# Layer 2 of a four-layer graph network: VectorE's compares of unit u + 2 ahead of its sum and add of unit u

## The chip, the cores and the metric

One core of a Trainium2 chip runs the whole program. The metric is the time of one execution on the device in microseconds (us), the median over runs. Engines are named as in the profile: PE is TensorE's matmul and PEld its weight load, DVE is VectorE, ACT is ScalarE, POOL is GpSimd and SP is SyncE; a q behind the name (PEldq, DVEq) marks what the engine's own instruction sequencer does, register work above all.

## The reference

A graph network of four layers over 6250 nodes and 206250 edges, 128 features for each node. The change touches layer 2 alone, a mean over neighbours:

```python
def _L2_gnn_ref(x, edge_index, Wl, bl, Wr, br):
    tgt, nbr = edge_index[0], edge_index[1]
    agg_sum = segment_sum(x[nbr], tgt, n)
    deg = segment_sum(ones(E), tgt, n)
    agg = agg_sum / maximum(deg, 1.0)[:, None]
    out = relu(x @ Wl + bl + agg @ Wr + br)
    ...
h = maximum(_layernorm(x), 0.0)
x = x + _L2_gnn_ref(h, edge_index, ...)
```

The kernel computes `agg_sum` and `deg` in `l2_edges`, as matrix products.

## The kernel before

The program is a row of phases with a barrier of all engines between them. The nodes lie in NB = 49 blocks of 128, and the edges are sorted into tiles of 128. A tile and a block that it touches make a meeting; there are NMEET = 4896 of them (padding included). `l2_edges` handles them in units of U = IG = 16 meetings with the same source block, so in 306 units, and a unit in two halves of H = 8. Its loop has 153 iterations of two units on each engine. `g` counts halves (612) and `u` units. Per unit:

- VectorE, `hot_of` (L2041): two compares of 128x2048 bf16 build 16 pairs of one-hot matrices, `hot_dst` and `hot_src`, from the edge ends in `ends_of`. Both tiles have two buffers. It raises `hot`.
- TensorE, `build` (L2014): for a half, 8 matmuls of a one-hot pair, 128x128 each, into PSUM `psM`. It raises `built`.
- ScalarE (L2003): one copy of a half from `psM` to `meets` in bf16. It raises `moved`.
- TensorE, `apply` (L2018 to L2025): one register load of 8 block numbers from `dst_blk` (L2018), then 8 matmuls of 390 columns with a block of `parts` each, whose address comes from a register; they add up in one bank of PSUM `psO`. It raises `summed`.
- VectorE: the sum of the three parts of the unit's `psO` bank into `sums` (L2060, it raises `joined`), and the add of `sums` onto the block of `agg` (L2064, it raises `added`). The block numbers for both units of an iteration are loaded from `src_blk` into VectorE's registers at the head of its loop (L2052).

The order of the work is written out by hand: each engine runs its own list in order, and semaphores join them. TensorE's list is build(g+1), apply(g), so its matmuls of a half are always built one half ahead of use. build(g+1) waits for `hot` when g+1 is the first half of a unit; apply(g) waits for ScalarE's copy of g, and in the first half of a unit for `joined`, so that the bank of `psO` is free. VectorE's list is, for unit u: compares of unit u+1, then sum of u, then add of u. The sum has to wait for `summed` of both halves of u.

No DMA runs in this phase: both number tables and `parts` are in SBUF.

Of the kernel before, what the change touches and what calls it, by code (L numbers as in the profile page):

```python
# [4 lines left out]
F32 = mybir.dt.float32  # L5
I32 = mybir.dt.int32
BF16 = mybir.dt.bfloat16
# [3 lines left out]
ENG = mybir.EngineType  # L11


P = 128
N, E, D = 6250, 206250, 128
HEADS, HEAD_DIM = 4, 32
NB = -(-N // P)
# [11 lines left out]
NTX = NT + 4 * HALF  # L29
# [4 lines left out]
QC = NPX // P  # L34
# [10 lines left out]
IG = 16  # L45
NMEET = 4896
JR = 40
NJ = JR * P
TPP = NTX // P
XW = D + 2  # L50
assert NMEET % (2 * IG) == 0 and NMEET >= NTX + (NB - 1) * NB + (IG - 1) * NB and NJ >= NMEET + IG and NTX % P == 0 and QC * 2 == TPP
LN_EPS = 1e-5
assert (P * ET - E) <= HALF * P and NH % 2 == 0 and NPX % P == 0 and ET * P >= E + 2 * P
BLOCK_RANGE = "block numbers are clamped to 0..NB-1 where they are made"
# [5 lines left out]
def fresh(kind):  # L60

    _names[0] += 1
    return f"{kind}_{_names[0]}"
# [41 lines left out]
def bc(ap, shape):  # L105
    return ap.broadcast_to(shape)


def flat(ap):
    return ap.rearrange("p a b -> p (a b)")  # L110


def gnn_kernel(nc, ins, out):
# [24 lines left out]
    with es:  # L138
# [27 lines left out]
        with nc.sbuf_tensor([P, NB, W], F32) as agg:  # L166
            c["agg"] = agg
            l1_finish(nc, c, ins, table1, running, last_pairs)
            with nc.sbuf_tensor([P, 2, NJ], BF16) as ends_of, nc.sbuf_tensor([1, NJ], I32) as dst_blk, nc.sbuf_tensor([1, NJ // IG], I32) as src_blk:
                l2_lists(nc, c, qtab, tile_rows, starts, meet_rows, ends_of, dst_blk, src_blk)  # L170
                with nc.sbuf_tensor([P, NB, 3, XW], BF16) as parts:
                    l2_nodes(nc, c, parts)
                    l2_edges(nc, c, ends_of, dst_blk, src_blk, parts)
            l2_finish(nc, c, ins)
# [1802 lines left out]
def l2_edges(nc, c, ends_of, dst_blk, src_blk, parts):  # L1977

    es = ExitStack()
    sb = lambda shape, dt=F32: es.enter_context(nc.sbuf_tensor(fresh("buf"), shape, dt))
    sem = PhaseSemaphores(nc)
    es.callback(sem.give_back)
    agg = c["agg"]
    U, H = IG, IG // 2
    with es:
        iota, sums = sb([P, P, 2], BF16), sb([P, 2, XW])
        hot_dst, hot_src = sb([P, 2, U // 2, P, 2], BF16), sb([P, 2, U // 2, P, 2], BF16)
        meets = sb([P, 2, H, P], BF16)  # L1990
        psM = es.enter_context(nc.psum_tensor(fresh("psum"), [P, 2, H, P], F32))
        psO = es.enter_context(nc.psum_tensor(fresh("psum"), [P, 2, 512], F32))
        numbered, hot, built, moved, summed, joined, added = (sem() for _ in range(7))
        with nc.Block() as block:
            @block.scalar
            def _(act):
                act.sem_inc(moved, 2)
                with act.Fori(0, NMEET // (2 * U)) as i:
                    for h in range(4):
                        g = 4 * i + h  # L2000
                        act.wait_ge(built, g + 1)
                        act.wait_ge(summed, g + 1)
                        nc.scalar.copy(meets[:, h % 2].rearrange("p a k -> p (a k)"), psM[:, h % 2].rearrange("p a k -> p (a k)")).then_inc(moved, 1)  # L2003

            @block.tensor
            def _(pe):
                def build(g, h, u):
                    if h % 2 == 0:
                        pe.wait_ge(hot, u + 1)
                    pe.wait_ge(moved, g + 1)  # L2010
                    b = (h // 2) % 2
                    for k in range(H):
                        at = H * (h % 2) + k
                        last = nc.tensor.matmul(psM[:, h % 2, k, :], hot_dst[:, b, at // 2, :, at % 2], hot_src[:, b, at // 2, :, at % 2], start=True, stop=True)  # L2014
                    last.then_inc(built, 1)

                def apply(g, h, u, i):
                    blocks = nc.values_load_multi_w_load_instructions(  # L2018
                        dst_blk[0:1, bass.ds(2 * U * i + H * h, H)], engines=[ENG.PE], min_val=0, max_val=NB - 1,
                        skip_runtime_bounds_check_because=BLOCK_RANGE)[1]  # L2020
                    pe.wait_ge(moved, g + 3)
                    if h % 2 == 0:
                        pe.wait_ge(joined, u + 1)
                    for k in range(H):
                        last = nc.tensor.matmul(psO[:, (h // 2) % 2, 0:3 * XW], meets[:, h % 2, k, :], parts[:, bass.ds(blocks[k], 1), :, :].rearrange("p b w d -> p (b w d)"),  # L2025
                                                start=(h % 2 == 0 and k == 0), stop=(h % 2 == 1 and k == H - 1))
                    last.then_inc(summed, 1)

                pe.sem_inc(summed, 2)
                build(0, 0, 0)  # L2030
                with pe.Fori(0, NMEET // (2 * U)) as i:
                    for h in range(4):
                        g = 4 * i + h
                        build(g + 1, h + 1, 2 * i + (h + 1) // 2)
                        apply(g, h, 2 * i + h // 2, i)

            @block.vector
            def _(dve):
                def hot_of(b, at):
                    for to, w in ((hot_dst, 0), (hot_src, 1)):  # L2040
                        last = nc.vector.tensor_tensor(to[:, b], bc(iota[:].unsqueeze(1), [P, U // 2, P, 2]),  # L2041
                                                       bc(ends_of[:, w, at].rearrange("p (a t) -> p a t", t=2).unsqueeze(2), [P, U // 2, P, 2]), ALU.is_equal)
                    last.then_inc(hot, 1)

                dve.sem_inc(added, 1)
                dve.sem_inc(joined, 2)
                nc.vector.memset(agg[:], 0.0).then_inc(added, 1)
                nc.vector.tensor_copy(iota[:], bc(c["iota"][:].unsqueeze(2), [P, P, 2])).then_inc(numbered, 1)
                dve.wait_ge(numbered, 1)
                hot_of(0, slice(0, U))  # L2050
                with dve.Fori(0, NMEET // (2 * U)) as i:
                    blocks = nc.values_load_multi_w_load_instructions(  # L2052
                        src_blk[0:1, bass.ds(2 * i, 2)], engines=[ENG.DVE], min_val=0, max_val=NB - 1,
                        skip_runtime_bounds_check_because=BLOCK_RANGE)[1]
                    for h in range(2):
                        u = 2 * i + h
                        dve.wait_ge(built, 2 * u)
                        hot_of((h + 1) % 2, bass.ds(2 * U * i + U * (h + 1), U))
                        dve.wait_ge(summed, 2 * u + 4)
                        nc.vector.tensor_reduce(sums[:, h, :], psO[:, h, 0:3 * XW].rearrange("p (w d) -> p d w", w=3), AX.X, ALU.add).then_inc(joined, 1)  # L2060
                        dve.wait_ge(joined, u + 3)
                        dve.wait_ge(added, u + 2)
                        a = flat(agg[:, bass.ds(blocks[h], 1), 0:D + 1])
                        nc.vector.tensor_tensor(a, a, sums[:, h, 0:D + 1], ALU.add).then_inc(added, 1)  # L2064
# [568 lines left out]
```

## Time and profile before

| | us |
|---|---|
| median of 3 runs | 11218.07 |
| lowest and highest | 11213.9, 11227.5 |
| the profiled execution | 11216.49 |
| its span, first to last instruction | 11214.7 |
| the layer 2 edge phase, 6530 to 8622 us of the span | 2092.0 |
| TensorE busy in it | 1428.16 |
| VectorE busy in it | 978.34 |
| ScalarE busy in it | 619.51 |

The span is that of one profiled execution, and all rows come from it. TensorE's granted clock is given as a share of 2.4 GHz; a single stretch is at one of two levels, 1.0 (2.4 GHz) or 0.5 (1.2 GHz), and a mean lies between them.

### The profile page before, as it was taken

The numbers are of one execution on the slowest core, as the hardware profiler recorded it, in microseconds if no ns is written. First come the engines' busy times: TensorE is split into PE (matmuls) and PEld (weight loads), VectorE is DVE, ScalarE is ACT, GpSimd is POOL, SyncE is SP. The second block draws the span as 40 slices with busy tenths as digits, with TensorE's granted clock in tenths as the row PEclk, the third lists the DMA queues.
The fourth block names the chain that finished last, engine by engine and source line by source line (L and its number), as shares of the span: only waits on it lengthen the run. The fifth ranks groups of instructions, "written<-read, shape, count | busy, mean of one in ns | idle before, by whom it ended". The sixth has DMA issues, their size and how long they took to land. (4 is left out here: it accounts for less than half of the span.)

```text
span 11214.7 us, 161449 instructions
## 1 busy us (share of the span) xinstructions
PE 7016.7 (63%) x46023; PEld 5941.3 (53%) x46024; DVE 6329.4 (56%) x14524; ACT 2694.6 (24%) x4442; POOL 5210.9 (46%) x5267
## 2 busy tenths in 40 slices
PE   0034334443567658878787456666666588888885
PEld 0033333333466646666666334444444588888885
DVE  8932222222577766666666444444445566666665
ACT  5022222222455532222222132222222100000000
POOL 0057777777100057777777300000000477777773
PEclk5566666666678779999999779989898566666665
DMA  4045545545444445555555500000000333333335
GB/s 153 0 144 157 157 155 158 157 155 168 116 111 114 110 127 149 154 156 148 154 149 156 96 10 0 0 0 0 0 0 1 83 103 107 103 104 107 103 105 86
DMA packets 1150492, 1136.52 MB, mean 101 GB/s; under 512 B 239363, under 2 KB 959825, under 8 KB 1150117
## 3 DMA queue, kind: packets, MB, share of 16 engines
q1 hardware_dynamic: 948422, 666.82, 21.2%
q0 software_dynamic: 195904, 465.66, 15.2%
q10 hardware_dynamic: 6048, 2.84, 0.1%
q14 instruction: 89, 0.73, 0.0%
q8 instruction: 29, 0.48, 0.0%
HBM read 731.30 MB, written 403.51 MB: 101 GB/s over the span
## 5 line engine op out<-in xcount | busy, mean ns | idle before, releaser
L1028 POOL DMA_INDIRECT buf<-node_rows,buf x1728 | 1743.9, 1009 | 527.4 <-issue 526.2
L1522 POOL DMA_INDIRECT buf<-node_rows_ln,buf x1728 | 1711.4, 990 | 561.2 <-issue 496.9
L694 POOL DMA_INDIRECT edge_rows_by_src<-buf x1728 | 1692.6, 979 | 551.5 <-issue 526.4
L1058 PE MATMUL psum<-buf 128*128 128x128 f32 x1728 | 375.3, 375 | 1296.5 <-DVE buf L1021 1293.6
L2025 PE MATMUL psum<-parts,buf 128*128 x4896 | 1068.1, 368 | 141.4 <-issue 97.0
L2175 POOL IOTA buf<- 49x1 f32 x1 | 0.1, 124 | 2244.4 <-POOLq L821 2244.4
L1058 PEld LDWEIGHTS psum<-buf 128*128 128x128 f32 x1728 | 304.8, 199 | 1316.8 <-issue 1316.8
L2003 ACT CAST buf<-psum 128x1024 bf16<-128x1024 f32 x612 | 619.5, 1012 | 1475.7 <-PE psum L2014 1475.7
L786 DVE COPY buf<-buf 128x32 int32<-128x32 int32 x108 | 20.1, 186 | 1465.7 <-DMA buf<-records_by_dst 1465.5
L2041 DVE TENSOR_TENSOR buf<-buf,ends_of 128x2048 bf16<-128x2048 bf16 x614 | 724.6, 1222 | 134.5 <-issue 134.4
L2014 PE MATMUL psum<-buf 128*128 128x128 bf16 x4904 | 431.9, 235 | 569.0 <-DVE buf L2041 569.0
L2025 PEld LDWEIGHTS psum<-parts,buf 128*128 128x128 bf16 x4896 | 513.3, 106 | 518.4 <-issue 332.8
L2405 PE MATMUL psum<-buf 128*128 128x5 f32 x3456 | 744.3, 353 | 50.1 <-ACT buf L2382 50.1
L2405 PEld LDWEIGHTS psum<-buf 128*128 128x128 f32 x3456 | 734.7, 327 | 64.1 <-ACT buf L2382 64.1
L2014 PEld LDWEIGHTS psum<-buf 128*128 128x128 bf16 x4904 | 344.0, 106 | 767.6 <-DVE buf L2041 688.4
L2060 DVE TENSOR_REDUCE buf<-psum 128x130 f32<-128x390 f32 x306 | 172.6, 564 | 921.5 <-PE psum L2025 921.5
L2413 PE MATMUL psum<-buf 128*128 128x132 f32 x3456 | 662.0, 377 | 27.1 <-DVE buf L2497 26.7
L2413 PEld LDWEIGHTS psum<-buf 128*128 128x128 f32 x3456 | 646.8, 288 | 29.0 <-issue 28.8
L1633 DVE TENSOR_TENSOR buf<-buf 128x512 f32<-128x512 f32 x432 | 298.5, 691 | 623.5 <-DMA buf<-node_rows_ln,buf 597.4
L1537 ACT ACTIVATE buf<-psum 128x512 f32<-128x512 f32 x432 | 257.9, 597 | 1542.1 <-PE psum L1572 1506.3
L1568 PE MATMUL psum<-buf 128*128 128x128 f32 x1728 | 293.7, 297 | 511.8 <-DVE buf L1633 511.0
L1584 PEld LDWEIGHTS psum<-buf 128*128 128x128 f32 x3456 | 485.8, 203 | 239.9 <-issue 239.9
(428 smaller groups left out, 14529.8 us busy)
## 6 DMA issues: line engine op xcount, KB each, us to landing
buf<-edge_rows_by_src SPq DMA_DIRECT2D x114, 1056.0 KB, 5.7
buf<-edge_rows_by_src SPq DMA_DIRECT2D x110, 1024.0 KB
buf<-in_edge_attr SPq DMA_DIRECT2D x864, 128.0 KB
running_weighted_sums<-buf SPq DMA_DIRECT2D x108, 544.0 KB, 3.5
buf<-loc_rows_by_src SPq DMA_DIRECT2D x110, 512.0 KB, 5.0
buf<-loc_rows_by_dst SPq DMA_DIRECT2D x110, 512.0 KB, 4.8
running_sums<-buf SPq DMA_DIRECT2D x108, 512.0 KB, 3.0
edge_rows_by_src<-buf SPq DMA_DIRECT2D x139, 260.0 KB, 2.7
```

The lines of the kernel that those rows point to most:

```text
L694: nc.gpsimd.indirect_dma_start(rows, bass.IndirectOffsetOnAxis(ap=at[:, h, t:t + 1], axis=0), st[:, h, t, :], None).then_inc(scattered[h], 16)
L1028: nc.gpsimd.indirect_dma_start(rows[:, t, 0:used], None, table, bass.IndirectOffsetOnAxis(ap=stage[:, t:t + 1], axis=0)).then_inc(sem, 16)
L1058: last = nc.tensor.transpose(psT[:, sg % 2, t * P:(t + 1) * P], oh[:, 4 * sg + t, :], c["ident"][:])
L1522: nc.gpsimd.indirect_dma_start(xn[:, j, t, :], None, table1, bass.IndirectOffsetOnAxis(ap=stage[:, j // 4, at:at + 1], axis=0)).then_inc(g ...
L1584: last = nc.tensor.matmul(psT[:, (j + 1) % 2, t * P:(t + 1) * P], hS[:, (j + 1) % 2, t * P:(t + 1) * P], w2[:], start=True, stop=True)
L1633: nc.vector.tensor_tensor(ea[:, g4], ea[:, g4], xn[:, g4], ALU.add).then_inc(partial, 1)
L2003: nc.scalar.copy(meets[:, h % 2].rearrange("p a k -> p (a k)"), psM[:, h % 2].rearrange("p a k -> p (a k)")).then_inc(moved, 1)
L2014: last = nc.tensor.matmul(psM[:, h % 2, k, :], hot_dst[:, b, at // 2, :, at % 2], hot_src[:, b, at // 2, :, at % 2], start=True, stop=True)
L2025: last = nc.tensor.matmul(psO[:, (h // 2) % 2, 0:3 * XW], meets[:, h % 2, k, :], parts[:, bass.ds(blocks[k], 1), :, :].rearrange("p b w d ...
L2041: last = nc.vector.tensor_tensor(to[:, b], bc(iota[:].unsqueeze(1), [P, U // 2, P, 2]), bc(ends_of[:, w, at].rearrange("p (a t) -> p a t", ...
L2405: last = nc.tensor.matmul(psS[:, q, :], oh[:, s, 2 * q + k, :], sel[:, b, 2 * q + k, :], start=(k == 0), stop=(k == 1))
L2413: last = nc.tensor.matmul(sums(q), oh[:, h, 2 * q + k, :], rows[:, h, 2 * q + k, :], start=(k == 0), stop=(k == 1))
```

## The change

Before its loop VectorE builds two units of one-hot matrices instead of one, and in the loop, at unit u, the compares are those of u + 2. These go into the buffers that unit u itself has used, so they wait until TensorE has built both halves of u (`built` at 2u + 2, where it was 2u). The sum and the add of u stand behind them, as the sum and the add of u stood behind the compares of u + 1. The number of buffers, R, is 2 as before; all other edits put R in place of a 2 and 2R in place of a 4. The list `ends_of` is read one unit further at the end, which the assertion covers; two compares more are issued in all.

```diff
-    U, H = IG, IG // 2
+    U, H, R = IG, IG // 2, 2
@@ block.vector
-                dve.sem_inc(joined, 2)
+                dve.sem_inc(joined, R)
...
                 hot_of(0, slice(0, U))
-                with dve.Fori(0, NMEET // (2 * U)) as i:
+                hot_of(1, slice(U, 2 * U))
+                with dve.Fori(0, NMEET // (R * U)) as i:
...
-                    for h in range(2):
-                        u = 2 * i + h
-                        dve.wait_ge(built, 2 * u)
-                        hot_of((h + 1) % 2, bass.ds(2 * U * i + U * (h + 1), U))
+                    for h in range(R):
+                        u = R * i + h
+                        dve.wait_ge(built, 2 * u + 2)
+                        hot_of((h + 2) % R, bass.ds(R * U * i + U * (h + 2), U))
                         dve.wait_ge(summed, 2 * u + 4)
                         nc.vector.tensor_reduce(sums[:, h, :], psO[:, h, 0:3 * XW]...
-                        dve.wait_ge(joined, u + 3)
+                        dve.wait_ge(joined, u + 1 + R)
```

The first place is VectorE's list ahead of its loop and the first unit in it. L2041 is `hot_of`; in the kernel after, lines behind it stand one further down (L2052 is L2053, L2060 is L2061, L2064 is L2065). What moved:

```order
 L2048 CAST buf<-buf 128x256
-L2041 TENSOR_TENSOR buf<-buf,ends_of 128x2048 x2
-L2051 UNCONDITIONAL_BRANCH
-L2051 ISA
-L2052 TENSOR_LOAD src_blk
-L2057 REGISTER_ALU
+L2041 TENSOR_TENSOR buf<-buf,ends_of 128x2048 x4
+L2052 UNCONDITIONAL_BRANCH
+L2052 ISA
+L2053 TENSOR_LOAD src_blk
+L2058 ISA
```

Two compares, those of unit 1, are now ahead of the loop, and so all compares in the loop belong to a unit later than before.

The second place is the first unit in the body of VectorE's loop, with the semaphores that rows wait for: sem_274 is `built`, sem_276 `summed`, sem_277 `joined`, sem_278 `added`. The kernel before:

```order
L2052 TENSOR_LOAD src_blk
L2057 REGISTER_ALU
L2041 ISA [waits sem_274]
L2041 TENSOR_TENSOR buf<-buf,ends_of 128x2048
L2041 ISA
L2041 TENSOR_TENSOR buf<-buf,ends_of 128x2048
L2059 REGISTER_ALU
L2060 TENSOR_REDUCE buf<-psum 128x130 [waits sem_276]
```

The kernel after:

```order
L2053 TENSOR_LOAD src_blk
L2058 ISA
L2041 ISA [waits sem_274]
L2041 TENSOR_TENSOR buf<-buf,ends_of 128x2048
L2041 ISA
L2041 TENSOR_TENSOR buf<-buf,ends_of 128x2048
L2060 REGISTER_ALU
L2061 TENSOR_REDUCE buf<-psum 128x130 [waits sem_276]
```

The rows are the same but for the register step that works out the value to wait for (L2057, now L2058), and what they stand for is not: the pair of compares is that of u + 2 instead of u + 1, and the value of `built` that the first row waits for is 2u + 2 instead of 2u.

TensorE's list is the same in both kernels. Its part from one build to the apply behind it (sem_275 is `moved`, sem_161 `hot`):

```order
L2009 REGISTER_ALU
L2014 MATMUL psum<-buf 128x128 [waits sem_275,sem_161]
L2014 MATMUL psum<-buf 128x128 x7
L2018 ISA
L2018 TENSOR_LOAD dst_blk
L2021 REGISTER_ALU
L2025 ISA [waits sem_275]
L2025 MATMUL psum<-parts,buf 128x390
```

Nothing moved here: the first matmul of a unit's build waits for `hot`, and the register load stands between a build and its apply.

## Rows read from the trace of the kernel before

**Rows 1.** The page: span, and granted clock in 40 slices.

```profile
span 11214.7 us, 161449 instructions
...
PEclk5566666666678779999999779989898566666665
```

**Rows 2.** The windows view of the layer 2 edge phase: length, busy time (instructions), clock, DMA.

```profile
core 0: us, PE busy (x) PEld busy (x) DVE busy (x) ACT busy (x) POOL busy (x), PEclk, DMA share, GB/s
6530.00:8622.00 2092.00, 1428.16 (x9800) 852.54 (x9800) 978.34 (x1228) 619.51 (x612) 0.00 (x0) 0.90 0.00 0
```

**Rows 3.** The view of waits in this phase: total us, times, longest.

```profile
ACT buf L2003 <- PE psum L2014: 1475.7, 611, 13.2
DVE buf L2060 <- PE psum L2025: 921.5, 306, 5.2
PEld psum L2014 <- DVE buf L2041: 688.4, 306, 51.5
PE psum L2014 <- DVE buf L2041: 569.0, 306, 51.2
```

**Rows 4.** The timeline of PE, 8182.5 to 8200 us: start, length, what, [idle before].

```profile
8183.47 1.50 PE L2025 MATMUL psum<-parts,buf 128*128 x8 [0.49 <-DVE buf L2060]
8186.78 0.63 PE L2014 MATMUL psum<-buf 128*128 128x128 bf16 x8 [1.81 <-DVE buf L2041]
8187.74 2.78 PE L2025 MATMUL psum<-parts,buf 128*128 x8 [0.33 <-issue]
8190.32 0.90 PE L2014 MATMUL psum<-buf 128*128 128x128 bf16 x8
8191.06 1.49 PE L2025 MATMUL psum<-parts,buf 128*128 x8
8194.00 0.63 PE L2014 MATMUL psum<-buf 128*128 128x128 bf16 x8 [1.46 <-DVE buf L2041]
8195.01 1.50 PE L2025 MATMUL psum<-parts,buf 128*128 x8 [0.38 <-issue]
8196.40 0.63 PE L2014 MATMUL psum<-buf 128*128 128x128 bf16 x8
8197.48 1.50 PE L2025 MATMUL psum<-parts,buf 128*128 x8 [0.45 <-DVE buf L2060]
```

**Rows 5.** The timeline of DVE, the same stretch.

```profile
8182.48 0.56 DVE L2060 TENSOR_REDUCE buf<-psum 128x130 f32<-128x390 f32 x1 [2.55 <-PE psum L2025]
8184.36 2.36 DVE L2041 TENSOR_TENSOR buf<-buf,ends_of 128x2048 bf16<-128x2048 bf16 x2 [0.89 <-issue]
8190.56 0.56 DVE L2060 TENSOR_REDUCE buf<-psum 128x130 f32<-128x390 f32 x1 [3.84 <-PE psum L2025]
8191.35 0.29 DVE L2064 TENSOR_TENSOR agg<-agg,buf 128x129 f32 x1 [0.23 <-DVE buf L2060]
8191.59 2.36 DVE L2041 TENSOR_TENSOR buf<-buf,ends_of 128x2048 bf16<-128x2048 bf16 x2
```

**Rows 6.** The timeline of PE, 7504 to 7508.2 us.

```profile
7504.56 0.63 PE L2014 MATMUL psum<-buf 128*128 128x128 bf16 x8 [1.81 <-DVE buf L2041]
7505.52 1.50 PE L2025 MATMUL psum<-parts,buf 128*128 x8 [0.33 <-issue]
7506.86 0.62 PE L2014 MATMUL psum<-buf 128*128 128x128 bf16 x8
7507.54 0.83 PE L2025 MATMUL psum<-parts,buf 128*128 x4
```

**Rows 7.** The view of source lines L2018, L2010 and L2009: PE's sequencer; durations in ns.

```profile
L2018 PEldq TENSOR_LOAD <-dst_blk x612: 587/590/601, 6533.2 to 8617.9; - x153
...
L2010 PEldq EVENT_SEMAPHORE  x307: 51/51/51, 6523.4 to 8614.5; - x154
...
L2009 PEldq ALU_OP  x306: 32/32/32, 6536.1 to 8614.5; - x153
```

**Rows 8.** The timeline of PE at the phase's start, 6535 to 6543 us.

```profile
6535.16 2.78 PE L2025 MATMUL psum<-parts,buf 128*128 x8 [0.44 <-ACT buf L2003]
6538.59 1.62 PE L2025 MATMUL psum<-parts,buf 128*128 x8
```

**Rows 9.** The view of source lines L2041, L2003 and L2025: minimum, median, maximum in ns.

```profile
L2041 DVE TENSOR_TENSOR buf<-buf,ends_of x614: 1215/1221/1227, 6530.4 to 8616.5; 128x2048 bf16<-128x2048 bf16 x154
...
L2003 ACT CAST buf<-psum x612: 1012/1012/1017, 6533.9 to 8614.8; 128x1024 bf16<-128x1024 f32 x153
...
L2025 PE MATMUL psum<-parts,buf x4896: 326/328/533, 6535.2 to 8619.9; 128*128 x196
```

More of the change, by code:

```diff
@@ L50 @@
 XW = D + 2
-assert NMEET % (2 * IG) == 0 and NMEET >= NTX + (NB - 1) * NB + (IG - 1) * NB and NJ >= NMEET + IG and NTX % P == 0 and QC * 2 == TPP
+assert NMEET % (2 * IG) == 0 and NMEET >= NTX + (NB - 1) * NB + (IG - 1) * NB and NJ >= NMEET + 2 * IG and NTX % P == 0 and QC * 2 == TPP
 LN_EPS = 1e-5
@@ L1985, in l2_edges @@
     agg = c["agg"]
-    U, H = IG, IG // 2
+    U, H, R = IG, IG // 2, 2
     with es:
-        iota, sums = sb([P, P, 2], BF16), sb([P, 2, XW])
-        hot_dst, hot_src = sb([P, 2, U // 2, P, 2], BF16), sb([P, 2, U // 2, P, 2], BF16)
+        iota, sums = sb([P, P, 2], BF16), sb([P, R, XW])
+        hot_dst, hot_src = sb([P, R, U // 2, P, 2], BF16), sb([P, R, U // 2, P, 2], BF16)
         meets = sb([P, 2, H, P], BF16)
         psM = es.enter_context(nc.psum_tensor(fresh("psum"), [P, 2, H, P], F32))
-        psO = es.enter_context(nc.psum_tensor(fresh("psum"), [P, 2, 512], F32))
+        psO = es.enter_context(nc.psum_tensor(fresh("psum"), [P, R, 512], F32))
         numbered, hot, built, moved, summed, joined, added = (sem() for _ in range(7))
@@ L1997, in _ @@
                 act.sem_inc(moved, 2)
-                with act.Fori(0, NMEET // (2 * U)) as i:
-                    for h in range(4):
-                        g = 4 * i + h
+                with act.Fori(0, NMEET // (R * U)) as i:
+                    for h in range(2 * R):
+                        g = 2 * R * i + h
                         act.wait_ge(built, g + 1)
@@ L2010, in build @@
                     pe.wait_ge(moved, g + 1)
-                    b = (h // 2) % 2
+                    b = (h // 2) % R
                     for k in range(H):
@@ L2018, in apply @@
                     blocks = nc.values_load_multi_w_load_instructions(
-                        dst_blk[0:1, bass.ds(2 * U * i + H * h, H)], engines=[ENG.PE], min_val=0, max_val=NB - 1,
+                        dst_blk[0:1, bass.ds(R * U * i + H * h, H)], engines=[ENG.PE], min_val=0, max_val=NB - 1,
                         skip_runtime_bounds_check_because=BLOCK_RANGE)[1]
@@ L2024, in apply @@
                     for k in range(H):
-                        last = nc.tensor.matmul(psO[:, (h // 2) % 2, 0:3 * XW], meets[:, h % 2, k, :], parts[:, bass.ds(blocks[k], 1), :, :].rearrange("p b w d -> p (b w d)"),
+                        last = nc.tensor.matmul(psO[:, h // 2, 0:3 * XW], meets[:, h % 2, k, :], parts[:, bass.ds(blocks[k], 1), :, :].rearrange("p b w d -> p (b w d)"),
                                                 start=(h % 2 == 0 and k == 0), stop=(h % 2 == 1 and k == H - 1))
@@ L2030, in _ @@
                 build(0, 0, 0)
[L2031 to L2035, printed above, removed]
+                with pe.Fori(0, NMEET // (R * U)) as i:
+                    for h in range(2 * R):
+                        g = 2 * R * i + h
+                        build(g + 1, h + 1, R * i + (h + 1) // 2)
+                        apply(g, h, R * i + h // 2, i)
             @block.vector
@@ L2050, in _ @@
                 hot_of(0, slice(0, U))
-                with dve.Fori(0, NMEET // (2 * U)) as i:
+                hot_of(1, slice(U, 2 * U))
+                with dve.Fori(0, NMEET // (R * U)) as i:
                     blocks = nc.values_load_multi_w_load_instructions(
-                        src_blk[0:1, bass.ds(2 * i, 2)], engines=[ENG.DVE], min_val=0, max_val=NB - 1,
+                        src_blk[0:1, bass.ds(R * i, R)], engines=[ENG.DVE], min_val=0, max_val=NB - 1,
                         skip_runtime_bounds_check_because=BLOCK_RANGE)[1]
-                    for h in range(2):
-                        u = 2 * i + h
-                        dve.wait_ge(built, 2 * u)
-                        hot_of((h + 1) % 2, bass.ds(2 * U * i + U * (h + 1), U))
+                    for h in range(R):
+                        u = R * i + h
+                        dve.wait_ge(built, 2 * u + 2)
+                        hot_of((h + 2) % R, bass.ds(R * U * i + U * (h + 2), U))
                         dve.wait_ge(summed, 2 * u + 4)
                         nc.vector.tensor_reduce(sums[:, h, :], psO[:, h, 0:3 * XW].rearrange("p (w d) -> p d w", w=3), AX.X, ALU.add).then_inc(joined, 1)
-                        dve.wait_ge(joined, u + 3)
+                        dve.wait_ge(joined, u + 1 + R)
                         dve.wait_ge(added, u + 2)
```

## The prediction

> **What bounds the kernel now.** The page first: TensorE's granted clock is between 0.7 and 0.9 in the slices of the layer 2 edge phase [rows 1]. That phase can be costed alone, since a barrier stands at both ends of it. The windows view gives it 2092.0 us, in which no engine is full: TensorE is busy for 1428 us, VectorE for 978, ScalarE for 620, and no DMA runs [rows 2]. So the engines wait for each other in a ring. The view of waits names the ring: TensorE's first build matmul of a unit waits 306 times for VectorE's compares, 569 us in all, and VectorE's sum waits 306 times for TensorE's apply, 922 us [rows 3]. (The first of those 306 holds some 51 us from the phase before; it is the "longest" of its row.)
>
> The timelines show the ring turn. A sum starts at 8190.56, the add follows, the compares of the unit after it run 8191.59 to 8193.95 [rows 5], TensorE's build starts at 8194.00, its apply at 8195.01 lasts 1.50 us [rows 4], and only then comes the next sum. VectorE stands still while TensorE works and TensorE stands still for 1.46 to 1.81 us per unit while VectorE works [rows 4]. The work of one iteration (two units) takes 13.62 us on average: the first apply matmul starts at 6535.2 and the last at 8619.9 [rows 9], which is 2084.7 us over 153 iterations.
>
> **The change part by part.**
>
> *The compares a unit earlier.* TensorE's build of unit u + 1 now needs compares that VectorE issued at unit u - 1. These wait for the second build of unit u - 1, which ends about when the apply ahead of it has ended, run for 2.4 us, and are needed only at build(2u + 2), three halves later. At 2.0 us or more a half that is 6 us for 2.4 us of work, or about 4 us when the sum and add of the unit before stand ahead. The wait of 569 us [rows 3] is therefore gone, if VectorE keeps pace.
>
> *Does VectorE keep pace?* From one sum's start to the end of the compares behind it: 8190.56 to 8193.95 is 3.39 us inside an iteration, and 8182.48 to 8186.72 is 4.24 us where the loop turns and loads block numbers (the 0.89 us of idle "issue") [rows 5]. Together 7.63 us for an iteration. That is the floor that VectorE sets: 153 x 7.63 = 1167 us. TensorE has to be compared with this.
>
> *What TensorE needs when it never waits for `hot`.* An iteration has four halves, from apply to apply.
> - Second half of a unit to first half of the next, loop not turning: 7505.52 to 7507.54, 2.02 us, without any wait, at the high clock [rows 6].
> - The same where the loop turns: 8195.01 to 8197.48, 2.47 us [rows 4].
> - First half to second half of a unit, twice: always blocked at the high clock now, so bounded. It has the same matmuls and the same register load. From below: 2.02 us, as in the first case. From above: the two pieces that the trace shows apart, 0.96 us from a build released late to its apply (7504.56 to 7505.52) and 1.34 us from an apply to the build behind it (7505.52 to 7506.86), 2.30 us [rows 6]. In the 0.96 us the register load has 0.59 us [rows 7] and four other sequencer steps share the rest, about 0.09 us each. This half has one step more than the 2.02 us case (L2009 and L2010 [rows 7], less the wait for `joined`), so I take 2.10 us.
>
> The sum: 2.02 + 2.47 + 2 x 2.10 = 8.69 us an iteration, 1330 us in all. This is above VectorE's 7.63, so TensorE becomes the bound, and within TensorE its sequencer and not its array. The idle of 0.33 us "issue" between build and apply is the register load, which starts only once the sequencer has passed the build [rows 6]; it is what is late next, and it stays.
>
> *The clock.* The phase's mean is 0.90 [rows 2], so about a fifth of it runs at 1.2 GHz. A half without a wait at that level takes 6535.16 to 6538.59, 3.43 us [rows 8], or 8187.74 to 8191.06, 3.32 us, against 2.0 to 2.1. The low stretches come in a phase in which TensorE stands still once a unit. In the new one, eight build matmuls within 0.63 us and eight apply matmuls within 1.50 us fill each half of 2.0 to 2.1 us, and leave TensorE idle for some 0.3 us at a time [rows 6]. I take the clock as high throughout. The Trainium skill speaks against a sure gain here: "TensorE: Matmul & The Clock Gate", section "A second HAM failure mode: psum-queue depth-cycling", tells of a kernel whose matmul groups with short idle between them kept its clock going up and down. By that page the clock would not settle, and the result would be the 1446 us of the first rival below and not the 1330 us that I take; the rows show low stretches now but no stretch with only short idle, so they don't decide it.
>
> *ScalarE and the other waits.* The copy takes 1.01 us [rows 9] and is needed 3 us after its build starts (0.96 us plus one half), while it can end about 1.7 us after (0.63 of build, 1.01, semaphores). Slack 1.3 us; it stays hidden. The `psO` bank's sum is needed two halves after the apply that ends a unit, and is made within 0.6 us of it, since the compares ahead of it have ended: they begin 0.9 us (1.9 where the loop turns) after the last sum began, and end at 3.39 or 4.24, against a unit of 4.12 or 4.57 (8.69 less 4.12). If that cover is gone, each 0.1 us of lateness costs nothing until 4 us have gathered. The two compares more at the start lie beside TensorE's first build, as unit 1's did before; the compares for units beyond the last run beside the last applies. Everything else in the diff is constants: 0 us.
>
> *Total.* 2085 - 1330 = 755 us less. Against the profiled execution of 11216.5 us (the median is 11218.1, 0.01% from it) this gives 10461, and I put **10460 us**. A check from the other view: 569 - 51 = 518 us of waits, and a fifth of 2092 us regained at a rate of (3.43 - 2.06) / 3.43 = 0.40, 167 us, make 685 us; the rest are matmul ends that the 569 does not count, since a blocked PE drains first (PEld, which drains sooner, shows 688 in place of 569 [rows 3]).
>
> **The rivals.**
>
> *The clock keeps falling.* If a fifth of the time stays at the low level, the phase is x = 1330 + 0.2 x 0.40 x, so 1446 us, and the time 10576. For it: the clock falls now at places with only 1.5 to 1.8 us of idle. The page named above tells of such a kernel. Against: such idle is what goes. 8%.
>
> *VectorE becomes the bound.* It has 8.69 - 7.63 = 1.06 us to spare in an iteration of four compares. Were those stretched from 1.22 to more than 1.49 us by an engine that now always reads beside them, VectorE would set the pace; at 1.75 us an iteration is 9.75 us, the phase 1492, the time 10623. Against: in 614 compares, with TensorE at work beside some and not others, the longest is 1.227 us [rows 9]. 4%.
>
> *Another wait takes the place, or the change moves nothing.* If build(2u + 2) were held by something of TensorE's own unit (its copy, its bank), the ring would be as long as now and the time 11218. The list of waits has no such entry at all [rows 3], and the slacks above are over 1 us. 3%.
>
> *Slower: the clock stays low.* If dense work kept TensorE at 1.2 GHz for the whole phase, four halves would take 4 x 3.43 = 13.72 us, and with the loop turn's 0.45 us unhidden 14.17: 2168 us, 83 more than now, time 11300. It decides from 13.62 us an iteration on. The stretch at 6535.16 ran low and the next half (6538.59, 1.62 us) already high [rows 8], so dense work brought the clock up, not down. 2%.
>
> *The halves that I bounded are better or worse.* Part of the forecast: 2.02 in both gives 8.53, 1305 us and 10436; 2.30 in both gives 9.09, 1391 us and 10522. The forecast, these bounds included, has 83%.
>
> **How the numbers follow.** 0.83 for 10436 to 10522, 0.08 for the clock (10576), 0.04 for VectorE (10623), 0.03 for no change, 0.02 for slower. About 0.2% (22 us) is what a measurement of this kernel can tell from none. The range is 10425 to 10545: the bounds, 10 us below them for a loop turn that is hidden in part, and 20 us above for some low stretches of the clock. Faster is 0.83 + 0.08 + 0.04 = 0.95, same 0.03, slower 0.02.
>
> **What would show it.** In the profile of the changed kernel: the wait of L2014 for L2041 near 0 but for its first; the mean clock of the phase above 0.97; first to second apply of a unit 2.1 us apart, an iteration 8.7 us; the sum's line waiting for TensorE for under 1 us a unit where it was 3; compares still 1.22 us; the phase 1330 to 1340 us long, all others unchanged. The prediction is wrong if the idle at L2025 grows (a register load slower beside a busy array), if L2025 waits for ScalarE's L2003, or if compares lengthen.

## The result, and the profile after

The changed kernel takes 10460.5 us (median of 4 runs, 10457.3 to 10469.9) against 11216.4 us before (4 runs), a ratio of 0.9326 with a 95% interval of 0.9310 to 0.9342. The forecast was 10460.

All of the gain is in the layer 2 edge phase. In this text "the phase" runs from the first apply matmul to the last, both of which stand in the view of the apply's source line (number of instructions: minimum, median and maximum ns, first and last start in us). After:

```profile
L2025 PE MATMUL psum<-parts,buf x4896: 325/328/533, 6542.4 to 7873.9; 128*128 x196
```

7873.9 - 6542.4 is 1331.5 us, where before it was 2084.7 [rows 9]; 753.2 us less. The spans of the two profiled executions are 10467.8 and 11214.7 us, 746.9 apart; outside the phase the new one took 6 us more (7.2 ahead of it, 0.9 less behind it), in phases that the change doesn't touch. The windows view of the whole phase after, with the columns of [rows 2]:

```profile
6537.00:7876.00 1339.00, 1209.94 (x9800) 790.91 (x9800) 981.24 (x1230) 619.26 (x612) 0.00 (x0) 1.00 0.00 0
```

VectorE and ScalarE do the same work as before to within 0.3%. TensorE has the same 9800 matmuls, but their busy time is down from 1428 to 1210 us, mainly because the granted clock is now 1.00 and no longer 0.90. The page shows the clock in its 40 slices of 262 us; the last five 9s of the row, slices 26 to 30, are this phase (9 stands for 90% or more):

```profile
span 10467.8 us, 161451 instructions
...
PEclk6566666666678887999999986999996666666665
```

The view of waits in the phase, against [rows 3]:

```profile
ACT buf L2003 <- PE psum L2014: 724.5, 611, 13.3
PEld psum L2025 <- issue: 228.8, 612, 0.7
DVE buf L2061 <- PE psum L2025: 164.1, 306, 1.6
DVE buf L2041 <- issue: 136.0, 152, 0.9
...
PE psum L2014 <- DVE buf L2041: 51.2, 1, 51.2
```

The 306 waits of the build for the compares have become one, the first, which began in the phase before. The sum waits for the apply for 0.54 us a unit and not for 3.01. What is left on TensorE is above all "issue" ahead of the apply's weight loads, 0.37 us in each of 612 halves: the register load. The timeline of PE shows one iteration without a single wait for VectorE's compares:

```profile
7204.57 1.50 PE L2025 MATMUL psum<-parts,buf 128*128 x8 [0.49 <-DVE buf L2061]
7205.91 0.62 PE L2014 MATMUL psum<-buf 128*128 128x128 bf16 x8
7206.67 1.50 PE L2025 MATMUL psum<-parts,buf 128*128 x8
7208.01 0.62 PE L2014 MATMUL psum<-buf 128*128 128x128 bf16 x8
7208.68 1.49 PE L2025 MATMUL psum<-parts,buf 128*128 x8
7210.01 0.62 PE L2014 MATMUL psum<-buf 128*128 128x128 bf16 x8
7210.80 1.49 PE L2025 MATMUL psum<-parts,buf 128*128 x8 [0.17 <-issue]
```

From apply to apply these are 2.10, 2.01 and 2.12 us. The fourth half, where the loop turns, is the one ahead of 7204.57; its 0.49 us are put down to L2061, but that sum was done by 7204.15, and it is the sequencer's turn of the loop and its register load. VectorE over the same stretch:

```profile
7203.59 0.56 DVE L2061 TENSOR_REDUCE buf<-psum 128x130 f32<-128x390 f32 x1 [0.68 <-PE psum L2025]
7204.29 0.30 DVE L2065 TENSOR_TENSOR agg<-agg,buf 128x129 f32 x1
7205.48 2.36 DVE L2041 TENSOR_TENSOR buf<-buf,ends_of 128x2048 bf16<-128x2048 bf16 x2 [0.89 <-issue]
7208.21 0.56 DVE L2061 TENSOR_REDUCE buf<-psum 128x130 f32<-128x390 f32 x1 [0.36 <-PE psum L2025]
```

The compares of 7205.48 run beside the applies of 7204.57 and 7206.67, where in [rows 4, 5] TensorE ran out of work in the middle of each pair of compares and stood still for 1.46 to 1.81 us.

### The profile page after: what moved, and what is told of

It reads as the page before. It is cut to its first block and busy times, and to the rows that moved or that the text cites. A ratio compares the mean times of both kernels' runs of the same rounds, so it can differ in the third digit from the quotient of the medians.

```text
span 10467.8 us, 161451 instructions
## 1 busy us (share of the span) xinstructions
PE 6804.7 (65%) x46023; PEld 5885.1 (56%) x46024; DVE 6330.8 (60%) x14526; ACT 2693.5 (26%) x4442; POOL 5212.0 (50%) x5267
## 5 line engine op out<-in xcount | busy, mean ns | idle before, releaser
L2025 PE MATMUL psum<-parts,buf 128*128 x4896 | 916.9, 329 | 124.3 <-DVE buf L2061 70.5
L2041 DVE TENSOR_TENSOR buf<-buf,ends_of 128x2048 bf16<-128x2048 bf16 x616 | 726.8, 1221 | 136.1 <-issue 136.0
L2003 ACT CAST buf<-psum 128x1024 bf16<-128x1024 f32 x612 | 619.3, 1012 | 724.5 <-PE psum L2014 724.5
L2025 PEld LDWEIGHTS psum<-parts,buf 128*128 128x128 bf16 x4896 | 471.9, 96 | 435.9 <-issue 228.8
L713 ACT COPY buf<-psum 128x512 f32<-128x512 f32 x432 | 253.5, 587 | 1395.0 <-PE psum L1058 1394.5
L1183 PE MATMUL psum<-buf 128*128 128x129 f32 x3456 | 530.3, 321 | 124.3 <-DVE buf L1256 124.3
L738 PE MATMUL psum<-buf 128*128 x3456 | 600.9, 332 | 0.8 <-ACT buf L713 0.8
```

Of the source, the lines that this page charges most:

```text
L738: last = nc.tensor.matmul(psX[:, g % 2, t // 2, (t % 2) * WT:(t % 2 + 1) * WT], ohT[:, g % 2, t * P:(t + 1) * P], flat(tab[:, bass.ds(bloc ...
L1183: last = nc.tensor.matmul(psA[:, half, q // 3, (q % 3) * W:(q % 3) * W + D + 1], oh[:, t, :], rows[:, s, t, 0:D + 1], start=(k == 0), stop ...
L2025: last = nc.tensor.matmul(psO[:, h // 2, 0:3 * XW], meets[:, h % 2, k, :], parts[:, bass.ds(blocks[k], 1), :, :].rearrange("p b w d -> p ( ...
```

## The experiments

Theory A: a ring of apply, sum, add, compares, build and apply set the time; the new order takes the compares out of it, and what is left is TensorE's own sequencer, with VectorE's floor 1.06 us an iteration below it. Rivals: the clock made most of the gain; VectorE is the bound now; the place of the compares in the list counts for itself, and not the ring.

The experiments ran on three chips. On two of them the phases with DMA took some 1.6 to 1.8 ms longer for every kernel (the kernel before: 12796 and 12965 us). The phase has no DMA, and where the changed kernel was run on a second chip its length was the same to within 0.6 us (below), so each experiment is read by its phase in its one profiled execution. On the chip with 12796 us, which ran the one compare behind, the fillers and the two edits of the register load, no unedited kernel was profiled; there the compares have the same length as elsewhere, 1.22 us.

### The changed kernel again

> The changed kernel once more, unedited, as the base of the other kernels on this chip, where the phases that move data by DMA can take another time. Both theories expect the layer 2 edge phase to measure the same here, 1331 us from the first apply to the last, 8.71 us an iteration, with the clock at 1.0.

12226.3 us (4 runs) against 12964.9 for the kernel before on that chip, ratio 0.9425 (0.9399 to 0.9452). Its apply line:

```profile
L2025 PE MATMUL psum<-parts,buf x4896: 326/328/533, 7655.4 to 8987.5; 128*128 x196
```

1332.1 us, within 0.6 us of the other chip. The ratio differs since the rest of the program is longer there; the time saved is 739 us there and 756 on the first chip. The seven runs of the kernel before on the second chip lie up to 67 us apart.

### One of the two compares behind the sum

```diff
-    hot_of((h + 2) % R, bass.ds(...))
+    hot_of((h + 2) % R, bass.ds(...), (0,))     # hot_dst
     dve.wait_ge(summed, 2 * u + 4)
     ... sum, add ...
+    hot_of((h + 2) % R, bass.ds(...), (1,))     # hot_src, raises hot
```

> The change half undone: of the two compares of unit u + 2 the one into hot_dst stands ahead of the sum and add of unit u, the one into hot_src behind them. Theory A (a ring through VectorE set the time, and the new order opens it): the second compare ends 1.03 + 1.22 = 2.25 us after the sum's start (3.1 us where the loop turns), while TensorE would start that build 1.8 us (2.3 us) after it in the changed kernel. So TensorE waits 0.5 and 0.8 us, and 0.2 us more each for the register load behind a late build: 1.7 us an iteration, 260 us in all, about 10720 us, with L2014 waiting for L2041 again. Rival (only the unit of lead in the buffers counts, not the place of the wait for summed): the lead is the same, so 10460.

12176.2 us (one run; before 12796.0). The phase is 9035.8 - 7582.2 = 1453.6 us, 122 more than the changed kernel, with the clock at 1.00. The wait is back, as the view of waits shows:

```profile
PEld psum L2014 <- DVE buf L2043: 169.5, 210, 51.5
PE psum L2014 <- DVE buf L2043: 100.7, 154, 51.2
```

So the lead in the buffers alone doesn't do it: the rival is out. But the price was half of my 260 us. The timeline of its VectorE, the first three rows at a place where the loop does not turn, the next three where it does:

```profile
8204.39 0.56 DVE L2064 TENSOR_REDUCE buf<-psum 128x130 f32<-128x390 f32 x1 [1.42 <-PE psum L2025]
8205.18 0.29 DVE L2068 TENSOR_TENSOR agg<-agg,buf 128x129 f32 x1 [0.23 <-DVE buf L2064]
8205.39 2.35 DVE L2043 TENSOR_TENSOR buf<-buf,ends_of 128x2048 bf16<-128x2048 bf16 x2
8209.21 0.56 DVE L2064 TENSOR_REDUCE buf<-psum 128x130 f32<-128x390 f32 x1 [1.46 <-PE psum L2025]
8209.92 0.29 DVE L2068 TENSOR_TENSOR agg<-agg,buf 128x129 f32 x1
8210.13 2.35 DVE L2043 TENSOR_TENSOR buf<-buf,ends_of 128x2048 bf16<-128x2048 bf16 x2
```

Where the loop turns, no 0.89 us of "issue" stands any more ahead of the compares: `hot_src` is the last thing in the body, and VectorE's register load runs beside it (from 8210.5 on, 0.53 us). I had charged the turn to the ring. A row of two compares holds `hot_src` of u + 2 and, right behind it, `hot_dst` of u + 3, 1.2 us each. So the compare that counts ends 2.2 us after the sum's start in the first place and 2.1 in the second. TensorE over the same stretch:

```profile
8204.86 1.50 PE L2025 MATMUL psum<-parts,buf 128*128 x8
8206.67 0.63 PE L2014 MATMUL psum<-buf 128*128 128x128 bf16 x8 [0.30 <-DVE buf L2043]
8207.67 1.50 PE L2025 MATMUL psum<-parts,buf 128*128 x8 [0.37 <-issue]
...
8210.14 1.50 PE L2025 MATMUL psum<-parts,buf 128*128 x8 [0.45 <-DVE buf L2064]
...
8212.40 1.50 PE L2025 MATMUL psum<-parts,buf 128*128 x8 [0.31 <-issue]
```

In the first place the build waits 0.30 us, and the register load behind the late build comes late as well: the half takes 2.81 us (8204.86 to 8207.67), 0.69 more than the 2.12 of the changed kernel. In the second the build's matmuls wait for nothing, and the half takes 2.26 us, 0.16 more than 2.10. That is about 0.8 us an iteration, the 122 us.

### The clock alone: filler matmuls in the kernel before

```diff
 def build(g, h, u, fill=0):
+    for k in range(fill):
+        nc.tensor.matmul(psF[:, 0:2 * P], iota[:, :, 0], flat(iota[:]), start=True, stop=True)
     if h % 2 == 0:
         pe.wait_ge(hot, u + 1)
 ...
-build(g + 1, h + 1, 2 * i + (h + 1) // 2)
+build(g + 1, h + 1, 2 * i + (h + 1) // 2, 10 if h % 2 else 0)
```

> The kernel before, with 10 filler matmuls of 256 columns into a spare PSUM bank ahead of each wait of a build for the compares, so that TensorE has work while it waits; their results are used by nothing. It tells the clock's share apart. Theory A (the ring is most of the gain, the low clock some of it): the clock goes to 1.0, an iteration to that of one without low stretches, 12.73 us, so 136 us less, 11080. Rival (most of the gain came from the clock): below 10800. If the fillers delay the build, up to 0.2 us a unit comes back, 11140.

12642.5 us (one run; before 12796.0). The phase is 9507.6 - 7558.4 = 1949.2 us, 135.5 less than the kernel before, 12.74 us an iteration. Its windows view and its timeline of PE:

```profile
7553.00:9509.00 1956.00, 1595.56 (x12860) 1066.12 (x12860) 978.95 (x1228) 619.55 (x612) 0.00 (x0) 1.00 0.00 0
```

```profile
8006.51 1.26 PE L2010 MATMUL psum<-buf 128*128 128x256 bf16 x10
8008.51 0.64 PE L2017 MATMUL psum<-buf 128*128 128x128 bf16 x8 [0.75 <-DVE buf L2044]
8009.48 1.49 PE L2028 MATMUL psum<-parts,buf 128*128 x8 [0.33 <-issue]
```

The fillers (L2010) end before the compares do, so they delay nothing; the build still waits for VectorE; and the mean clock of the phase is 1.00. The clock alone is therefore worth 136 of the 753 us, and the other 618 are the ring's.

### The sum done twice, after and before

```diff
+nc.vector.tensor_reduce(spare[:, h, :], psO[:, h, 0:3 * XW]..., AX.X, ALU.add)
 nc.vector.tensor_reduce(sums[:, h, :], psO[:, h, 0:3 * XW]..., AX.X, ALU.add).then_inc(joined, 1)
```

> The changed kernel with the sum of a unit done twice, the first time into a scratch tile that nothing reads: 0.56 us more for VectorE per unit. Theory A (TensorE is the bound, VectorE has 1.06 us to spare an iteration): VectorE's floor rises from 7.63 to 8.76 us, as much as TensorE's 8.71, so the phase grows by 10 to 30 us, not more. Rival (VectorE is on the path): 306 x 0.56 = 173 us more.

> The same second sum in the kernel before. Theory A (the sum is a part of the ring): all of it shows, 173 us more, and up to 30 us beyond that since TensorE stands still longer and its clock is low more often. Rival (VectorE was idle for 3 us a unit, so there is room): under 50 us more.

In the changed kernel: 12224.6 us (one run; the changed kernel itself 12226.3), the phase 8977.6 - 7645.3 = 1332.3 us, where 1332.1 was measured without them. Nothing of 306 more sums shows, not even the 10 to 30 us that I had expected. VectorE is now all but full, in the timeline:

```profile
8002.38 0.56 DVE L2061 TENSOR_REDUCE buf<-psum 128x130 f32<-128x390 f32 x1 [0.17 <-PE psum L2025]
8002.86 0.55 DVE L2062 TENSOR_REDUCE buf<-psum 128x130 f32<-128x390 f32 x1
...
8007.02 0.56 DVE L2061 TENSOR_REDUCE buf<-psum 128x130 f32<-128x390 f32 x1
```

The second sum starts 0.48 us after the first, so its price is 0.48 and not 0.56 us, and VectorE's floor is 7.63 + 0.96 = 8.59 us, just under TensorE's 8.70. The rival that VectorE sets the time is out, and its room is bounded from below: 0.96 us an iteration at least were free.

In the kernel before: 13015.4 us (one run; before 12964.9), the phase 9764.2 - 7625.8 = 2138.4 us, 54 more, and neither the 173 of theory A nor quite the rival's "under 50". The windows view tells why:

```profile
7621.00:9766.00 2145.00, 1328.78 (x9800) 796.67 (x9800) 1122.07 (x1533) 619.25 (x612) 0.00 (x0) 0.96 0.00 0
```

The clock is 0.96 here, above the 0.90 of [rows 2], although TensorE stands still for longer. Against the filled kernel, where the clock is 1.00, the phase is 189 us longer; 2 x 0.48 us in 153 iterations are 147 us of it, which leaves 42 for the low stretches. Two iterations of this kernel at a clock of 1.00, each row the first apply of one, bear the 147 out:

```profile
8001.14 1.50 PE L2025 MATMUL psum<-parts,buf 128*128 x8 [0.49 <-issue]
...
8014.80 1.50 PE L2025 MATMUL psum<-parts,buf 128*128 x8 [0.44 <-issue]
...
8028.59 1.50 PE L2025 MATMUL psum<-parts,buf 128*128 x8 [0.49 <-issue]
```

They take 13.66 and 13.79 us, about 1 us more than the 12.74 of the filled kernel. So the added sums are in the ring, and a change of the clock's pattern hid most of them in the difference of 54. Why the clock fell less often there is open.

### The register load: two of 4, or one of 16

The code is shortened: `values_load` stands for the kernel's long call that loads numbers into TensorE's registers, and the lines that it replaces are not shown.

```diff
 # two loads of 4
+for q in range(2):
+    blocks += values_load(dst_blk[0:1, bass.ds(R * U * i + H * h + H // 2 * q, H // 2)])
 # one load of 16
+if h % 2 == 0:
+    held[:] = values_load(dst_blk[0:1, bass.ds(R * U * i + H * h, U)])
+blocks = held[H * (h % 2):H * (h % 2) + H]
```

> The changed kernel, with TensorE's register load of a half split into two loads of 4 numbers. Theory A (the sequencer's load is on the path in each half): 0.65 us more in each of 612 halves, 400 us, 10860. Rival (loads are hidden behind the queued matmuls): 10460 to 10500.

> The changed kernel, but TensorE loads the 16 block numbers of a unit in one register load instead of 8 in each half. Theory A (TensorE's sequencer sets the pace now, and VectorE is 1 us an iteration behind): TensorE's iteration falls from 8.7 to 7.5 us, VectorE's floor of 7.63 takes over, 7.7 us with its waits: 155 us less, 10305. Rival 1 (TensorE's array or ScalarE's copy is the bound): 10460. Rival 2 (VectorE is the bound already): 10460, with VectorE hardly idle.

Two loads of 4: 12221.6 us (one run; before 12796.0), the phase 9061.2 - 7581.9 = 1479.3 us, 148 more. One load of 16: 11963.4 us (4 runs), ratio to before 0.9347 (0.9332 to 0.9363), the phase 8824.1 - 7567.0 = 1257.1 us, 74 less. Both move the time the way theory A says, and rule out an array or a ScalarE bound in the changed kernel. Both sizes were off by more than half, because I had taken a load for a lump, and its time goes by the registers it fills; for the one load a second bound comes in as well (below). The views of the source line, the changed kernel's first:

```profile
L2018 PEldq TENSOR_LOAD <-dst_blk x612: 588/592/600, 6540.5 to 7871.9; - x153
```

```profile
L2020 PEldq TENSOR_LOAD <-dst_blk x1224: 330/332/347, 7580.0 to 9059.4; - x175
```

```profile
L2021 PEldq TENSOR_LOAD <-dst_blk x306: 1102/1106/1114, 7565.1 to 8819.7; - x153
```

332, 592 and 1106 ns for 4, 8 and 16 registers: 65 ns a register and some 75 ns for the load. Two loads of 4 in place of one of 8 cost 72 ns more; the phase grew by 0.24 us a half, and the rest is put down to the sequencer's steps around a second load. One load of 16 in place of two of 8 saves 78 ns and such steps, and 0.24 us a unit as measured. In the half without a load TensorE's array is now the bound:

```profile
8003.53 1.50 PE L2029 MATMUL psum<-parts,buf 128*128 x8 [0.61 <-DVE buf L2065]
8004.87 0.62 PE L2014 MATMUL psum<-buf 128*128 128x128 bf16 x8
8005.33 1.49 PE L2029 MATMUL psum<-parts,buf 128*128 x8
8006.65 0.62 PE L2014 MATMUL psum<-buf 128*128 128x128 bf16 x8
8007.44 1.50 PE L2029 MATMUL psum<-parts,buf 128*128 x8 [0.17 <-DVE buf L2065]
```

1.80 us from the first apply to the second, with build and apply end to end, which is 0.30 less than the changed kernel's 2.10; and 2.11 to the third, where the load of 16 stands and the changed kernel took 2.01.

### Three buffers, in either order

```diff
-    U, H, R = IG, IG // 2, 2
+    U, H, R = IG, IG // 2, 3
 # the second kernel besides: compares behind the sum and add, three units ahead
+    hot_of(2, slice(2 * U, 3 * U))
 ...
-    dve.wait_ge(built, 2 * u + 2)
-    hot_of((h + 2) % R, bass.ds(R * U * i + U * (h + 2), U))
 ... sum, add ...
+    dve.wait_ge(built, 2 * u + 2)
+    hot_of(h, bass.ds(R * U * i + U * (h + R), U))
```

> The changed kernel with R = 3: three one-hot buffers, three psO banks, three units in an iteration; the compares stay two units ahead. Theory A (TensorE's sequencer sets the pace, no buffer is short): only 51 of 153 loop turns of 0.47 us go, 24 us less. Rival (buffers or VectorE's turn hold the phase): over 60 us less.

> VectorE's order of the kernel before (sum, add, then compares), but with three buffers, so that the compares behind the sum of unit u are those of u + 3. Theory A (only the ring matters: compares must not stand between the end of a unit and the next build that needs them): the build that needs them is 6 us after the sum, the compares end 3.4 to 4.2 us after it, so the phase is that of the three-buffer kernel in the new order, 1301 us. Rival (compares must stand ahead of the sum to be in time): the phase stays near the kernel before, above 1900 us.

In the new order: 12164.8 us (4 runs; the changed kernel 12226.3), ratio to before 0.9380 (0.9352 to 0.9408), the phase 8939.0 - 7638.4 = 1300.6 us, 31 less where 24 were expected. With the compares last, as in the kernel before, and a third buffer: 10449.3 us (one run; before 11224.2), the phase 7851.0 - 6549.6 = 1301.4 us, the same. Its view of waits:

```profile
DVE buf L2060 <- PE psum L2025: 266.7, 306, 3.0
PEld psum L2025 <- issue: 202.9, 614, 0.7
...
PE psum L2014 <- DVE buf L2041: 51.2, 1, 51.2
```

One wait for the compares, the first, in an order in which they stand behind the sum. So the place of the compares has no worth of its own; what counts is that they are not on the way from the end of a unit to the next build. A third buffer takes them out of that way as well as the swap does; that it is 30 us faster goes with the loop's turns, 102 in place of 153, since the new order gains the same from it.

### Both edits together

> The changed kernel with R = 3 and one register load of 16 block numbers per unit on TensorE, the two edits that each gave something alone (74 us and 31 us of the phase). A unit should take 1.80 + 2.08 us and a loop turn 0.47 us: 12.1 us for an iteration of three units, the phase 1234 us, 98 less than the changed kernel. VectorE's floor is near it: 3 x 3.39 + 0.85 = 11.0 us. Rival: VectorE or the array is the bound by now, and the phase stays at 1257 us.

10367.5 us (4 runs) against 11224.2 for the kernel before on that chip, ratio 0.9236 (0.9221 to 0.9252), so faster than the changed kernel too (0.9326, 0.9310 to 0.9342, on another chip). The phase:

```profile
L2029 PE MATMUL psum<-parts,buf x4896: 325/328/533, 6543.0 to 7773.7; 128*128 x196
```

1230.7 us, where 1234 were expected. The halves add up as they had been measured apart.

## Why the prediction was right

- **The ring.** The wait of L2014 for L2041 was to go, and it did, from 306 waits to the first one. Half undone (one compare behind the sum) it comes back; with a third buffer the old order loses it as well.
- **TensorE's sequencer as the next bound.** The sum was 2.02 + 2.47 + 2 x 2.10 = 8.69 us an iteration. Measured: 1331.5 / 153 = 8.70. The two halves of 2.10, which the trace of before never showed without a wait at the high clock, are 2.10 and 2.12 in the timeline. The other two, 2.02 and 2.47, measured 2.01 and 2.46 (7206.67 to 7208.68 and 7210.80 to 7213.26). Changing only the register loads moves the phase by 148 us up or 74 down, so the sequencer is the bound; with the load out of a half, that half fell from 2.10 to 1.80 us, which is the array's floor. My argument for it spoke of the load as a lump; the price is by the register, which did not enter the sum, since the load was left as it was.
- **VectorE keeps pace.** Its floor of 7.63 us held: 0.96 us an iteration more cost nothing. One reading in that part was off: inside an iteration the compares begin 1.03 us after the sum (8190.56 to 8191.59 in [rows 5]) and not 0.9; nothing else was worked out from it.
- **The clock.** It was taken as high throughout, and is 1.00. The check in the prediction gave the clock 167 of the 755 us; the filled kernel shows 136. That term was too large: the low time was right (410 us by the windows view of the kernel before in steps of 0.5 us, for my 418), but a low microsecond cost 0.33 and not 0.40. TensorE was busy in some 400 of the 410 us, so it was not spent on waiting; part of it fell on the apply that runs beside VectorE's compares. The one that starts at 6640.51 in the trace of the kernel before took 1.86 us instead of 1.50, and the build behind it had to wait for compares that ended at 6644.14 all the same. The Trainium skill's section "A second HAM failure mode: psum-queue depth-cycling" ("TensorE: Matmul & The Clock Gate") tells of a kernel whose clock went up and down with short pauses between its groups of matmuls. This case does not agree: with 0.2 to 0.5 us of idle between groups the clock of the changed kernel is 1.00 over the 1331 us.
- **The rivals.** None came about. The check from the waits (685 us) fell short of the 753 although its clock term was 31 too large: its waits came to 518 us where the ring was worth 618. In the half-undone order a wait of 0.30 us came with 0.39 more behind it, so listed waits alone count too little.

The forecast was 10460 and the measurement 10460.5. That closeness owes something to chance: the phase was 1.9 us off (1331.5 for 1329.6), and the rest of the program differs by 6 us between the two profiled executions. The four runs lie 13 us apart.

The expectations of single experiments missed more often, and each miss was a size: the half-undone order (122 for 260 us, because the loop turn hides behind a compare that stands last), the loads (148 for 400 and 74 for 155, because a load goes by its registers, and because the array takes over at 1.80 us in a half without one), the doubled sum in the kernel before (54 for 173, because the second sum adds 0.48 us and not 0.56 and the clock's pattern moved).

## What to carry to other kernels

When two engines in one loop take turns, follow the ring from the end of a unit to the next one and ask of each piece of work in it whether it has to stand there. Work that depends only on old data can be moved out by order or by one more buffer, whichever is cheaper; here each took away all waits but the first. Then cost the other engines' floors from stretches without a wait, at the clock that they will have, since the next bound decides what the edit is worth, and a register load inside a loop can be that bound.

## What the runs showed of the hardware that was not expected

- A load of block numbers into TensorE's registers takes 332, 592 and 1106 ns for 4, 8 and 16 of them, about 65 ns each and some 75 ns besides.
- VectorE's register load at a loop turn costs 0.89 us of idle where the work ahead of it has a short tail (the add), and nothing where a 1.2 us compare stands last, as in the half-undone order and in the three-buffer kernel with the compares last.
- More idle on TensorE does not have to mean a lower mean clock: 0.90 in the kernel before with TensorE idle for 664 us of the phase, 0.96 with the doubled sum and 816 us idle, an iteration of 14.0 us instead of 13.6. The cause is open.
- The program outside this phase took 1.6 to 1.8 ms longer on two of the chips, for all kernels, while the phase, which has no DMA, agreed within 0.6 us on the one of them where the same kernel was profiled.
